# Norms with tokens on partitions, one-instruction outputs of three attentions, and plain scatters in the routed experts of layer 1

## The reference, cut to what matters

```python
h = layernorm(x) * (1 + ca) + sa
x = x + ga * attention(h)
h = layernorm(x) * (1 + cb) + sb
x = x + gb * ffn(h)
```

```python
for e in range(N_EXPERTS):
    h = new_gelu(xf @ Wfc[e] + bfc[e]) @ Wproj[e] + bproj[e]
    routed = routed + h * gate[:, e:e + 1]
```

## Time and profile before

| | |
|---|---|
| median of 3 runs | 3533.31 us (3531.64 to 3540.31) |
| the profiled execution | 3533.18 us, of which its span is 3530.9 us |
| PE busy | 2712.3 us (77%), 20859 instructions |
| DVE busy | 2145.8 us (61%), 5390 instructions |
| ACT busy | 1307.7 us (37%) |
| POOL busy | 983.5 us (28%), 1089 instructions |
| mean granted clock of PE | 0.882 |

### The profile page before, as it was taken

One profiled execution on the slowest core, in us unless ns is written; L12 is line 12 of the kernel. 1 busy time (PEld: TensorE's weight loads), 2 busy tenths in 40 slices (PEclk: granted clock), 3 DMA queues, 4 the chain that ended last, 5 costly groups with the idle time before them and its releaser, 6 DMA issues. The chain is left out here.

```text
span 3530.9 us, 69910 instructions
## 1 busy us (share of the span) xinstructions
PE 2712.3 (77%) x20859; PEld 1810.2 (51%) x20884; DVE 2145.8 (61%) x5390; ACT 1307.7 (37%) x2884; POOL 983.5 (28%) x1089
## 2 busy tenths in 40 slices
PE   5888624317887887679849987788879998997999
PEld 3666524305665664528725555566634474455444
DVE  5776672137888786512247775777555567846455
ACT  1566201003665565324316663356432222133221
POOL 2332106852334332265622322334200020011000
PEclk6999756557999999889959998799989999998999
DMA  3332302334433331316521110333100004400000
GB/s 74 52 49 35 129 36 53 48 77 57 54 44 49 49 46 14 145 60 127 92 68 27 24 23 7 50 46 48 38 2 1 0 6 96 96 7 25 5 0 24
DMA packets 164036, 165.85 MB, mean 47 GB/s; under 512 B 30472, under 2 KB 136720, under 8 KB 158736
## 3 DMA queue, kind: packets, MB, share of 16 engines
q1 hardware_dynamic: 128240, 138.50, 20.4%
q0 software_dynamic: 34336, 21.83, 4.4%
q10 hardware_dynamic: 1152, 1.61, 0.1%
HBM read 52.90 MB, written 33.01 MB: 24 GB/s over the span
## 5 line engine op out<-in xcount | busy, mean ns | idle before, releaser
L569 ACT ACTIVATE a1PR<-bank 128x384 f32<-128x384 f32 x512 | 242.4, 492 | 143.6 <-PE bank L626 140.7
L792 DVE TENSOR_REDUCE a1NM<-bank 128x3 f32<-128x384 f32 x512 | 263.0, 549 | 26.6 <-PE bank L608 24.6
L795 DVE TENSOR_REDUCE a2NMQ<-bank 128x2 f32<-128x512 f32 x256 | 168.1, 685 | 60.8 <-PE bank L612 60.6
L959 PE MATMUL bank<-ONES 128*128 128x256 bf16 x960 | 169.5, 283 | 26.4 <-DMA f1nWR<-in_wr 5.0
L569 ACT ACTIVATE a2PR<-bank 128x512 f32<-128x512 f32 x256 | 149.6, 596 | 91.3 <-PE bank L630 89.2
L792 DVE TENSOR_REDUCE a4NM<-bank 128x3 f32<-128x384 f32 x256 | 136.1, 552 | 57.0 <-PE bank L608 55.3
L792 DVE TENSOR_REDUCE a0NM<-bank 128x3 f32<-128x384 f32 x256 | 136.6, 553 | 50.2 <-PE bank L608 47.4
L624 PE MATMUL bank<-a1QH,a1KH 128*128 128x128 bf16 x512 | 115.6, 227 | 57.4 <-ACT a1PR L569 43.1
L569 ACT ACTIVATE a4PR<-bank 128x384 f32<-128x384 f32 x256 | 121.2, 489 | 97.5 <-PE bank L626 96.6
L569 ACT ACTIVATE a0PR<-bank 128x384 f32<-128x384 f32 x256 | 119.9, 489 | 82.7 <-PE bank L626 82.0
L2208 POOL DMA_INDIRECT routed<-yY,yID x80 | 123.6, 1545 | 85.7 <-DMA routed<-yY,yID 41.4
(11 more groups left out here) (675 smaller groups left out, 8334.9 us busy)
## 6 DMA issues: line engine op xcount, KB each, us to landing
lVB<-lV SPq DMA_DIRECT2D x64, 256.0 KB
yWT<-in_w SPq DMA_DIRECT2D x40, 256.0 KB, 3.0
a1QH<-a1SPL SPq DMA_DIRECT2D x96, 64.0 KB
a1KH<-a1SPL SPq DMA_DIRECT2D x96, 64.0 KB
a1QH<-a1QH SPq DMA_DIRECT2D x96, 64.0 KB
a1KH<-a1KH SPq DMA_DIRECT2D x96, 64.0 KB
rows_by_slot<-gZB SPq DMA_DIRECT2D x5, 1040.0 KB
yXG<-rows_by_slot SPq DMA_DIRECT2D x40, 130.0 KB, 3.1
```

The lines of the kernel that those rows point to most:

```text
L569: nc.scalar.activation(PR[:, h % 8, :], bank[2 + h % 2][:, 0:NC], ACT.Exp, scale=SCALE)\
L792: v.tensor_reduce(NM3[:, h, :], S_BANK[h % 3][:, 0:NC].rearrange("p (n k) -> p n k", n=3), AX, ALU.max, negate=True).then_inc(s_used.sem, 1)
L795: v.tensor_reduce(NMQ[:, :, h], S_BANK[h % 3][:, 0:NC].rearrange("p (n k) -> p n k", n=2), AX, ALU.max, negate=True).then_inc(s_used.sem, 1)
L959: pe.matmul(bank[7][:, 0:2 * P], spare[:, 0:P], spare[:, :], start=True, stop=True)
```

## The change

It has three parts.

1. `norm_phase` is written anew. It takes 8 groups of 512 tokens. PE transposes a group to tokens on partitions (L959 of the new file; four transposes into PSUM), DVE takes mean and variance of each token by `bn_stats` (L1020) and `bn_aggr` (L1024), and VE (L1040) and POOL give the power -1/2 for four columns at once. DVE normalizes two of the four quarters (L1032) and ACT the other two, PE transposes back (L969), and ACT applies scale and shift on the way to the destination. The router's matmul (L978) reads the destination. The constant matmuls are gone, and PE and ACT wait for the small loads only where these are used.
2. In attentions without output bias (a0, a1, a4) one instruction (`scalar_tensor_tensor`, or `tensor_tensor` in a4) adds the scaled bank to the residual. a2 is as before.
3. The routed experts write Y to rows of their own instead of adding: row 80*128 + token + 4096 * choice, or, for an unused row, a row of its own below 80*128. POOL no longer waits for the scatter before, the accumulators need no zeros, and four semaphores free the buffers of Y and ID2.

```diff
-                    ctt_ready=1, ctt_copied=1, o_ready=1, tmp_ready=1, x_updated=1)
+                    ctt_ready=1, ctt_copied=1, o_ready=1, tmp_ready=1, x_updated=int(bool(cfg.get("bo"))))
...
                             after(v, o_ready, b)
-                            after(v, x_updated, b - 1)
                             if cfg.get("plain"):
-                                v.tensor_copy(TMP[:, :], bank[7][:, 0:T]).then_inc(tmp_ready.sem, 1)
+                                v.tensor_tensor(DST[:, tok(b)], bank[7][:, 0:T], DST[:, tok(b)], ALU.add).then_inc(tmp_ready.sem, 1)
+                            elif not cfg.get("bo"):
+                                v.scalar_tensor_tensor(DST[:, tok(b)], bank[7][:, 0:T], c.MOD[:, l, 2, one(b)], DST[:, tok(b)],
+                                                       ALU.mult, ALU.add).then_inc(tmp_ready.sem, 1)
                             else:
+                                after(v, x_updated, b - 1)
                                 v.tensor_scalar(TMP[:, :], bank[7][:, 0:T], COL[:, 1:2], c.MOD[:, l, 2, one(b)],
                                                 ALU.add, ALU.mult).then_inc(tmp_ready.sem, 1)
-                            after(v, tmp_ready, b)
-                            v.tensor_tensor(DST[:, tok(b)], DST[:, tok(b)], TMP[:, :], ALU.add).then_inc(x_updated.sem, 1)
+                                after(v, tmp_ready, b)
+                                v.tensor_tensor(DST[:, tok(b)], DST[:, tok(b)], TMP[:, :], ALU.add).then_inc(x_updated.sem, 1)
...
+    place = lambda g, n: (EVEN_BANK[g % 3] if n < 2 else ODD_BANK[g % 2])[:, n % 2 * P:(n % 2 + 1) * P]
...
-                for _ in range(n):
-                    pe.matmul(bank[7][:, 0:2 * P], spare[:, 0:P], spare[:, :], start=True, stop=True)
...
+            for t in range(NG + 4):
+                g = t
+                if g < NG:
+                    after(pe, xv, g - 3)
+                    for n in range(4):
+                        if n == 2:
+                            after(pe, xa, g - 2)
+                        mm = pe.transpose(place(g, n), SRC[:, g * F + n * P:g * F + (n + 1) * P], c.ID)
+                        if n % 2:
+                            mm.then_inc(turned_in.sem, 1)
+                g = t - 2
+                if 0 <= g < NG:
+                    after(pe, xv, g)
+                    after(pe, hr, g - 2)
+                    for n in range(4):
+                        if n == 2:
+                            after(pe, xa, g)
+                        mm = pe.transpose(OUT_BANK[g % 2][:, n * P:(n + 1) * P], XN[:, g % 2, n, :], c.ID)
+                    mm.then_inc(turned_out.sem, 1)
+                g = t - 4
+                if E and 0 <= g:
+                    if g == 0:
+                        pe.wait_ge(w_in, 16 * len(loads))
+                    after(pe, hr, g)
+                    after(pe, lg, g - 1)
...
+                nc.gpsimd.tensor_tensor(RS[:, g % 2, :], VE[:, g % 2, :], c.HALF[:, 0:4], ALU.pow).then_inc(rs.sem, 1)
...
+                    for n in (2, 3):
+                        made = nc.scalar.activation(XN[:, g % 2, n, :], place(g, n), ACT.Identity,
+                                                    bias=NR[:, g % 2, n:n + 1] if centered else 0.0, scale=RS[:, g % 2, n:n + 1])
+                    made.then_inc(xa.sem, 1)
+                g = t - 3
...
+                    for n in range(2):
+                        scale, shift = gains(2 * g + n)
+                        nc.scalar.activation(NT[:, tok(2 * g + n)], OUT_BANK[g % 2][:, n * T:(n + 1) * T], ACT.Identity, bias=shift, scale=scale)\
+                            .then_inc(hr.sem, 1)
...
+                    for n in range(4):
+                        if n % 2 == 0:
+                            after(v, turned_in, g, n // 2 + 1)
+                        v.bn_stats(ST[:, n, :], place(g, n)).then_inc(st.sem, 1)
+                    after(v, xv, g - 2)
+                    for n in range(4):
+                        after(v, st, g, n + 1)
+                        v.bn_aggr(MV[:, g % 2, n, :], ST[:, n, :]).then_inc(mv.sem, 1)
+                g = t - 1
+                if 0 <= g < NG:
+                    after(v, rs, g)
+                    after(v, xa, g - 2)
+                    v.scalar_tensor_tensor(NR[:, g % 2, :], MV[:, g % 2, :, 0], -1.0, RS[:, g % 2, :], ALU.mult, ALU.mult).then_inc(nr.sem, 1)
...
+                    for n in (0, 1):
+                        made = v.tensor_scalar(XN[:, g % 2, n, :], place(g, n),
...
-                for a in range(2):
-                    rows = ACC[a].rearrange("(p n) d -> p (n d)", p=P)
-                    for k in range(2):
-                        sp.dma_start(rows[:, 2112 * k:2112 * k + 2112], ZB[:, :]).then_inc(sums_zero, 16)
...
-                for a in range(2):
-                    sp.wait_ge(added[a], ADDED0 + 16 * TILES)
+                for k in range(4):
+                    sp.wait_ge(scattered[k], 8 * TILES)
...
-                        if j:
-                            pool.wait_ge(added[a], ADDED0 + 16 * j)
-                        nc.gpsimd.indirect_dma_start(ACC[a][:, :], bass.IndirectOffsetOnAxis(ID2[:, j % 4, a:a + 1], 0), Y[:, j % 4, a, :], None,
-                                                     bounds_check=DUMMY + NTOK - 1, oob_is_err=True, compute_op=ALU.add).then_inc(added[a], 16)
+                        nc.gpsimd.indirect_dma_start(OUT[:, :], bass.IndirectOffsetOnAxis(ID2[:, j % 4, a:a + 1], 0), Y[:, j % 4, a, :], None,
+                                                     bounds_check=DUMMY + 2 * NTOK - 1, oob_is_err=True).then_inc(scattered[j % 4], 16)
...
-                            for a in range(2):
-                                v.wait_ge(added[a], ADDED0 + 16 * (j - 3))
-                        v.tensor_scalar(ID2[:, j % 4, :], XG[:, j % RING, :, D], TAB[:, N + TILES:N + TILES + 1], None, ALU.max)
+                            v.wait_ge(scattered[j % 4], 32 * (j // 4))
+                        v.tensor_tensor(ID2[:, j % 4, :], XG[:, j % RING, :, D], TAB[:, N + TILES + 2 * j:N + TILES + 2 * j + 2], ALU.max)
```

More of the change, by code:

```diff
@@ L928, in norm_phase, with gains @@
             + ([(COL[:, 1:2], cfg["nshift"])] if cfg.get("nshift") else []) + ([(WR[:, :], cfg["wr"])] if E else [])
[L929 to L938, removed]
+        def gains(b):
+            if cfg.get("ngain"):
+                return COL[:, 0:1], (COL[:, 1:2] if cfg.get("nshift") else 0.0)
+            l, k = cfg["layer"], cfg["nmod"]
+            return c.MOD[:, l, k + 1, one(b)], c.MOD[:, l, k, one(b)]
         block = ctx.enter_context(nc.Block())
@@ new lines, in _ @@
+            for t in range(NG + 4):
[24 more added lines that the diff above has]
+                    for n in range(4):
+                        mm = pe.matmul(LG_BANK[:, n * E:(n + 1) * E], NT[:, g * F + n * P:g * F + (n + 1) * P], WR[:, :],
@@ L988, in step @@
                                        start=True, stop=True)
                     mm.then_inc(logits.sem, 1)
-            steps(pe, step)
         @block.gpsimd
         def _(pool):
-            def step(t, m):
-                if has(-1, t):
-                    d = (m - 1) % 2
-                    after(pool, ve, t - 1)
-                    after(pool, dg, t - 3)
-                    nc.gpsimd.tensor_tensor(RS[:, d, :], VE[:, d, :], c.HALF[:, 0:2], ALU.pow).then_inc(rs.sem, 1)
-            steps(pool, step)
+            for g in range(NG):
+                after(pool, ve, g)
+                after(pool, xv, g - 2)
+                after(pool, nr, g - 2)
+                nc.gpsimd.tensor_tensor(RS[:, g % 2, :], VE[:, g % 2, :], c.HALF[:, 0:4], ALU.pow).then_inc(rs.sem, 1)
@@ L1002, in _ @@
         @block.scalar
         def _(act):
-            def step(t, m):
-                if has(0, t):
-                    if centered:
-                        after(act, xc, t)
-                    after(act, var, t - 2)
-                    nc.scalar.activation(SQ[:, m % 2, :], XC[:, m, :] if centered else SRC[:, tok(t)], ACT.Square).then_inc(sq.sem, 1)
-                if has(-4, t):
-                    after(act, hr, t - 4)
-                    nc.scalar.copy(NT[:, tok(t - 4)], H[:, m % 4, :]).then_inc(copied.sem, 1)
@@ L1013, in _ @@
-            steps(act, step)
+            for t in range(1, NG + 3):
+                g = t - 1
+                if g < NG:
+                    after(act, nr, g)
+                    after(act, turned_out, g - 2)
+                    for n in (2, 3):
[3 more added lines that the diff above has]
+                g = t - 3
+                if 0 <= g:
+                    if g == 0 and loads:
+                        act.wait_ge(w_in, 16 * len(loads))
+                    after(act, turned_out, g)
+                    for n in range(2):
+                        scale, shift = gains(2 * g + n)
```

(7 more changed lines are left out.)

128 lines of the change are left out of this document (39 added, 89 removed).

## The result

The changed kernel takes 3396.61 us (median of 4 runs, 3388.49 to 3401.01) against 3533.56 us: ratio 0.9607, 95% interval 0.9584 to 0.9629. The forecast was 3371. The profiled execution took 3401.01 us (span 3399.2, mean clock 0.848 against 0.882), so its gain is 132 us where I had summed 162.

A forecast was written before the change was run, and what follows sets the result against it. No engine is busy throughout; PE has the largest share, 77% of the span, and bounds inside a norm. Norms 118 + loop 41.6 + attention 5 - clock 3 = 162 us off 3533.2: 3371 us, whole range 3320 to 3435.

The forecast's parts named there:

- The new norm without a router: Norms without a router: 8 groups of 2.4 us plus head and tail, 23.7 us each.
- Rivals 2 and 5: Norms: 2, bn_stats makes two passes, 70 us more, 8%; 5, bn_stats and bn_aggr run as long instructions, slower overall, 3%.
- Without a router the half clock costs nothing: Norms without a router: PE's 8 transposes, 2.2 us a group at half clock, stay under DVE's 2.4.
- DVE, not PE, is busy nearly throughout: New norms: a sign that the forecast holds, beside bn_stats near 0.3 us.
- The router norms: Four norms with a router: 27.2 us each, 108.8 us in all.
- With a router the tail has the logits and their copy (2.0): End of a norm with a router: logits and their copy add 2.0 us to the tail.
- Such a PE is busy without a pause, and the old norms show that it is then granted the full clock: Norms with a router: PE's first groups, 3.7 us each at half clock; 1.5 us charged for the way to full clock.
- Rival 1: Norms with a router: half-clock PE bounds all groups at 3.7 plus 0.2 us, 48 us more, 3419; 15%.
- The clock behind the norms: f4's experts and i3's linear attention start with PE at a lower clock: 2 and 1, 3 us more.
- The routed loop: Routed experts: plain scatters end the waits, a tile takes 3.73 us, the sums' loads start 41.6 us earlier.
- Rival 3: Routed loop: it keeps a wait, a tile stays at 4.09 us, 13 us more, 3384; 10%.
- The attention outputs: a0, a1 and a4: one output instruction instead of two, taken as 5 us less, between 1.5 and 25.

The follow-up runs named there:

- norm_only: The kernel before with the new norm alone: ratio 0.9721 to the kernel before.
- earlier_logits: The changed kernel with a group's router matmuls three steps behind instead of four, and ACT's write before a later normalizing: ratio 0.9550 to the kernel before.
- fill_router: The changed kernel with constant matmuls put back into the four norms with a router: ratio 0.9572 to the kernel before.
- one_copy_fill: The changed kernel with earlier_logits' order, one copy of all logits at the end in f1, f2, f3, and fill_router's constant matmuls: ratio 0.9549 to the kernel before.
- free_add: The changed kernel with scatters that add instead of write, without waiting for each other, onto rows zeroed beforehand: ratio 0.9606 to the kernel before.
- scat_only: The kernel before with the plain scatters alone: ratio 0.9890 to the kernel before.

## Why the prediction was right, and which step of it failed

**The new norm without a router: right in its time, partly by luck.** One bn_stats takes 0.282 us, and four in a row 0.89 (4 x 0.28 = 1.12 taken); four bn_aggr 0.36 (0.48), the two normalizing instructions 0.72 (0.52). POOL's power of 4 columns took 1.006 (1.0). Rivals 2 and 5 are out: one pass, and a pair at 0.31 (1.25 over 4). But the group's 2.44 us in h2 (2.4) are not DVE's own: DVE was busy for 2.0 of them (16.09 over 8), where the sum has 2.3, and waited for the rest, where it has 0.1. "Without a router the half clock costs nothing" was wrong, since PE's transposes at half clock are in the ring that DVE waits for: the last group of norm_only's i3 took 1.84 us at full clock. The sign "DVE, not PE, is busy nearly throughout" did not show either (8.18 of 10 us, PE 8.25). At the ends two errors cancel as well: the first two groups of h2 follow after 1.28 and 2.03 us, and from the last statistics to the end it was 7.4 us where the sum has 2.4 + 3.5.

**The router norms: the step that failed.** "With a router the tail has the logits and their copy (2.0)" counts one group's router matmuls behind the last statistics. PE's order puts them four steps behind, so five groups' stand there, 2.1 to 3.0 us apart at half clock in f3. That they run at half clock is the second half of the step: "Such a PE is busy without a pause, and the old norms show that it is then granted the full clock". In f3 PE had no pause and the clock stayed at 0.50. A group took 3.30 us there, so the prediction's own sign of being wrong, a group over 3 us, came in the router norms. Together the four norms take 129.1 us instead of 108.8: 20 of the 30 us by which the sum missed the profiled time. Rival 1 named the mechanism; its size, 48, was too large because a group took 3.3 us, not 3.9, and the first four groups have no router matmuls in them and keep 2.4 us or less. The shares can be read in f2: 32.3 us in the changed kernel, 30.5 with earlier_logits' order and 30.2 with one copy as well, all three at clock 0.50, and 22.9 with the constant matmuls added, at 0.93, which is 4 under my forecast. There the clock was the larger part. The Trainium skill (TensorE: Matmul & The Clock Gate, "What's actually happening") says that activity releases the throttle. The trace agrees for the loop (60 us busy, at 1.00); it does not for f3 (10 us busy, at 0.50), if busy rows are taken for activity, and these runs don't settle whether they may be.

**The clock behind the norms: right in sum**, 2.9 for 3, with f4's stage at 1.2 (2 taken) and i3's at 1.7 (1 taken).

**The routed loop: right.** The tile is at 3.73, and the waits are gone. Of the 41.6 us, 4.2 are missing: the first two tiles took 10.7 us instead of 8.1, at half clock (2.6), and from the last tile's first matmul to the loads it was 11.3 instead of 9.9 (1.4): the sum has the last tile's two scatters alone, and the two of the tile before stand ahead of them, 1.27 us apart. Rival 3 is out. Its 13 us were too few besides: the 4.09 us of a late tile are one of the shorter intervals, and the last 25 of the kernel before average 4.8. The runs add that either half of the edit would have kept the tile at 3.73.

**The attention outputs: right in sum by luck, not in place.** I took 5 and the profile has 6.1. Over all profiles a0 and a4 gain (a0 292.4 to 293.3 in three with old outputs, 287.4 to 290.8 in eleven with new; a4 303.5 to 306.9 and 296.0 to 303.2), and a1, from whose rows I had reasoned, doesn't (600.5 to 607.5 and 598.8 to 610.0): DVE still waits 1.46 us for PE before the output.

**The rest** is a2, 5.1 us longer with the same instructions, and 2 us in the norms without a router.

## What to carry to other kernels

When a pipeline's order says "four steps behind", count what is left in the queue when the last input is done, at the clock that will then hold; that tail is paid in every phase. Constant matmuls that look like waste can be what holds the clock: before they go, work out which stretches PE bounds at half clock, and try them there one by one, since f2 gained 7.3 us by them, and f3, in the same kernel, took 33.3 us with them and 28.4 and 30.3 without. When an engine's own work fits the measured step, look whether it is busy for all of it: h2's group had the time of the sum and another cause. Where a slow step can be made cheaper in two ways, each may be enough by itself; try them apart.

## What the runs showed of the hardware

- PE without a pause can stay at half clock. In f3 it was busy for 10.00 of 10 us with transposes and router matmuls, at 0.50; in f2 of fill_router, with two constant matmuls beside each group, for 7.94 of 10, at 1.00. Transposes alone, with pauses, had 1.00 late in norm_only's i3, busy for 1.82 of 3.2 us. f3 of one_copy_fill had 0.60 on the whole in spite of its constant matmuls. What decides it stays open.
- The same instructions of a2 took 310.9 to 311.1 us in the three profiles with old outputs of the other attentions and 314.2 to 323.1 in the eleven with new ones. Two of the 14, whole:

```profile
1817.23:2128.11 310.88, 277.99 (x2500) 170.21 (x2500) 230.71 (x497) 196.72 (x395) 84.76 (x140) 0.95 0.14 23
```

```profile
1765.66:2088.81 323.15, 287.72 (x2500) 175.00 (x2500) 231.43 (x497) 196.73 (x395) 84.72 (x140) 0.92 0.13 22
```

  The difference goes with the clock, 0.95 and 0.92. Early in a2 it rises either 27 to 28 us after the first score matmul (7 profiles) or 36 to 37 (7), and not always late with new outputs. Why kernels with new outputs of a0, a1 and a4 should fare worse in a2 stays open. A gain of 5 us in one attention can't be read from one profile.
- ACT needs 454 ns for 128 columns from PSUM with bias and scale by partition, and 364 in f2, where the bias is a constant; DVE's counterpart 403 and 343.
- An indirect scatter that adds holds POOL for 1.55 us, one that writes for 0.97, with or without waits around them. In the loop the first landed after 3.4 us before and 3.9 in free_add, the second after 3.0 in scat_only (medians).
